# Second cross-attention layer of a two-layer perceiver block: where the full steps issue their value, key and context products

## What is computed

```python
# query = layernorm(x): (2, 256, 256); key = value = ctx_1024: (2, 4096, 256)
Q = proj(query, wq, bq); K = proj(key, wk, bk); V = proj(value, wv, bv)   # 16 heads of 16
energy = einsum('bhqd,bhkd->bhqk', Q, K) / sqrt(16)
attn = softmax(energy, axis=-1)
out = einsum('bhqk,bhkd->bhqd', attn, V)
x = x + out.reshape(B, S, 256) @ wo.T + bo
```

## Time and profile before

| | us |
|---|---|
| median of three runs | 1801.49 |
| the profiled execution's own time | 1800.53 |
| its span | 1798.8 |
| PE busy | 1561.7 |
| DVE busy | 1071.2 |
| ACT busy | 744.7 |
| POOL busy | 503.4 |

### The profile page before, as it was taken

How to read it: one execution, slowest core, us unless ns; L and a number is a source line. 1 busy time by engine, 2 the same in 40 slices (tenths; PEclk the granted TensorE clock), 3 DMA queues, 4 the chain that set the end, 5 groups by cost and what they waited for, 6 DMA issues and landing times. The chain is left out here.

```text
span 1798.8 us, 26051 instructions
## 1 busy us (share of the span) xinstructions
PE 1561.7 (87%) x9943; PEld 1153.8 (64%) x9943; DVE 1071.2 (60%) x1684; ACT 744.7 (41%) x996; POOL 503.4 (28%) x630
## 2 busy tenths in 40 slices
PE   7989999999999668859999687999999899984298
PEld 6767777777877457738888554555565455442288
DVE  6856666666552564345665598777776776016641
ACT  4535555544544132223443111555455455852120
POOL 1005534434569000000000300544444444730000
PEclk9989999999999776759999898999999999996599
DMA  4333333322321100022222122111111110000253
GB/s 164 146 95 100 118 132 104 129 88 90 106 65 42 36 1 1 0 72 94 93 71 92 47 94 94 71 71 48 48 71 71 48 71 1 2 1 24 94 189 103
DMA packets 68527, 134.24 MB, mean 75 GB/s; under 512 B 8722, under 2 KB 38980, under 8 KB 68420
## 3 DMA queue, kind: packets, MB, share of 16 engines
q1 hardware_dynamic: 68228, 132.74, 22.5%
q10 hardware_dynamic: 192, 0.05, 0.0%
HBM read 98.64 MB, written 17.30 MB: 64 GB/s over the span
## 5 line engine op out<-in xcount | busy, mean ns | idle before, releaser
L850 ACT ACTIVATE P<-score 128x1024 f32<-128x1024 f32 x256 | 255.3, 1023 | 169.8 <-PE score L1262 169.8
L641 POOL CAST st<-ef 32x512 fp32r<-32x512 f32 x384 | 235.7, 614 | 313.0 <-PE score L1262 268.7
L1843 DVE TENSOR_REDUCE mx<-bank 128x1 f32<-128x512 f32 x384 | 247.3, 686 | 103.4 <-PE bank L1277 101.9
L1051 PE MATMUL bank<-c_hi,w_split 128*128 128x512 f32 x512 | 178.1, 411 | 19.4 <-ACT arena L947 5.9
L1262 PE MATMUL score<-qs,st 97*128 97x512 f32 x512 | 173.9, 429 | 5.0 <-DMA qs<-shift 3.8
L606 POOL TENSOR_TENSOR sum<-sum,P 128x512 f32<-128x512 f32 x84 | 111.6, 1329 | 192.5 <-ACT P L764 192.5
L764 ACT ACTIVATE P<-score 128x1024 f32<-128x1024 f32 x128 | 129.4, 1025 | 74.1 <-PE score L1087 71.7
L1277 PE MATMUL bank<-ef,qm 128*128 128x512 f32 x384 | 142.3, 431 | 18.5 <-DVE mx L1843 13.7
L1733 DVE TENSOR_REDUCE mx<-bank 128x1 f32<-128x512 f32 x192 | 123.5, 686 | 52.2 <-PE bank L1101 43.9
L1051 PE MATMUL bank<-w_split,c_hi 128*128 128x256 f32 x768 | 147.3, 291 | 0.6 <-ACT v L860 0.6
L1051 PEld LDWEIGHTS bank<-c_hi,w_split 128*128 128x128 f32 x512 | 99.0, 193 | 58.4 <-issue 13.3
(11 more groups left out here) (329 smaller groups left out, 2683.9 us busy)
## 6 DMA issues: line engine op xcount, KB each, us to landing
c_hi<-split_ctx SPq DMA_DIRECT2D x48, 512.0 KB, 3.3
c_lo<-split_ctx SPq DMA_DIRECT2D x48, 512.0 KB, 4.3
w<-k SPq DMA_DIRECT2D x128, 128.0 KB, 3.5
arena<-in_L_ffn_w SPq DMA_DIRECT2D x16, 1024.0 KB, 5.2
arena<-in_L_ffn_W SPq DMA_DIRECT2D x16, 1024.0 KB, 5.4
c_in<-in_ctx SPq DMA_DIRECT2D x16, 512.0 KB, 3.9
split_ctx<-c_hi SPq DMA_DIRECT2D x16, 512.0 KB, 3.6
split_ctx<-c_lo SPq DMA_DIRECT2D x16, 512.0 KB, 4.5
```

What stands on the lines that cost most here:

```text
L641: pool.tensor_copy(st1[32 * block:32 * block + 32, k, :], ef1[rows, g % ERING, part, :].bitcast(F32)).then_inc(a[f"st{k}"], 16)
L850: act.activation(P1[:, index % PRING, :], score[n % 2][:], ACT.Exp).then_inc(a["p"], 1)
L1051: last = mm(dst, l, r, start=(n == 0), stop=(n == len(pairs) - 1))
L1843: v.tensor_reduce(mx1[:, u % 2, i, n:n + 1], bank_of(a, g + 1, f"m{n}")[:], AX.X, ALU.max).then_inc(a["red"], 1)
```

## The change

In the full steps the mixture is issued in two rows of four blocks: row 1 takes the last four blocks of chunk `g - 1`, row 5 the first four of chunk `g`. All six key products come behind row 0, with ACT's copy behind its first weights and DVE's low part behind the reductions of row 1. The values come behind the rows 2 and 4, with ACT's copies behind its third and fifth weights. The instructions are the same in number and size; the steps before 9 and after 32 are as before, and so are the ends of the steps with `i = 0`.

```diff
@@ ACT, cross1
                         weights(g, n)
                         if i and t < CHUNKS:
-                            if n == 3:
+                            if n == 0:
                                 keys(t)
-                            if n in (5, 7) and u % 2 == 0:
-                                values(u, i, n // 2 - 2)
+                            if n in (2, 4) and u % 2 == 0:
+                                values(u, i, n // 2 - 1)
@@ PE, cross1
                         if t <= CHUNKS:
                             maxima(t - 1, n)
-                            if n < 2 and g % NCH:
-                                mixture(g - 1, (4 + 2 * n, 5 + 2 * n))
-                            if n in (4, 6):
-                                mixture(g, (n - 4, n - 3))
+                            if n == 1 and g % NCH:
+                                mixture(g - 1, range(4, 8))
+                            if n == 5:
+                                mixture(g, range(4))
...
                         if i and t < CHUNKS:
-                            if n in (2, 3):
-                                keys(t, (n - 2,))
-                            if n in (5, 7) and u % 2 == 0:
-                                values(t, n // 2 - 2)
+                            if n == 0:
+                                keys(t)
+                            if n in (2, 4) and u % 2 == 0:
+                                values(t, n // 2 - 1)
@@ DVE, cross1
-                        if (t < LAG and h == 1) or (i and LAG <= t < CHUNKS and h == 4):
+                        if (t < LAG and h == 1) or (i and LAG <= t < CHUNKS and h == 1):
                             low_keys(t)
```

## The result

The changed kernel takes 1822.2 us (median of four runs, 1813.69 to 1823.91) against 1800.8 for the kernel before: ratio 1.0108, 95% interval 1.0075 to 1.0141. It is slower, by 21.4 us where 15.4 were forecast; the median lies at the upper end of the range, 0.2 us above it. The profiled execution took 1822.17, its span is 1820.5.

The account below looks back on a forecast made before the run. How PE's rows line up with DVE's reductions through two banks of maxima bounds the kernel, not any engine's sum. Row prices summed over the stage gave 15.4 us on 1800.5, so 1816 us, range 1805 to 1822.

Parts of the forecast that it names:

- The cause: Full steps: merging two mixture rows saves 0.29 us if the emptied row needn't wait; it waits 0.70 or 0.32.
- The prices of rows: PE's rows in full steps: four blocks 2.99 us, whole keys 2.32, values 2.36, empty 1.66 behind filled, 1.28 behind empty.
- The sum of the full steps: All gains and losses of the stage's steps, from row 1 to row 1, added up: 15.4 us slower.
- Low parts of queries: DVE's work behind row 7's reductions, 1.68 us: delays steps by 0.67, against 0.90 before without values, 0.22 with them.
- Behind a division: Behind steps 17 and 25 DVE's division, 6.6 us, sets the time to the next row 1 before and after alike.
- The steps 15, 23 and 31: They end in row 0 of a step without keys there, 1.04 us less: in all -1.2 us.
- the steps 16 and 24: Rows 1 to 7 take 11.86 us against 10.96 before, 0.9 us lost in each.
- the clock, "So I count nothing": PE's short stops of 0.3 to 0.7 us in the steps leave the granted clock full: nothing added.
- faster rival: Full steps: DVE keeps ahead, emptied rows take 0.96 us, 45 mergers save 0.29 each, 13 us: 1787 us; chance 0.08.
- clock rival: Runs of three empty rows drop the clock once in each of 14 steps, 3.4 us each: 1863 us; chance 0.03.

Follow-up runs that it names:

- the parts alone: Kernel before with only the mixture in fours, 1823.6 us; or with only keys, values and low part of the keys moved, mixture in pairs, 1828.7 us.
- faster reductions: DVE's reductions of maxima in full steps cut to 256 of 512 columns: kernel before 1778.2 us, changed kernel 1774.9 us.
- a third bank: Changed kernel, but in steps without values maxima may also use the bank of the keys and values, order of instructions unchanged: 1798.0 us.
- the old order with a third bank: Kernel before, but in steps without values maxima may also use the bank of the keys and values in some rows: 1784.4 us.
- the seam filled: Eight small zero products behind the scores of each of rows 0 to 3 of step 33: changed kernel 1817.8 us, old order with a third bank 1784.5.
- the mixture alone: Kernel before with only the mixture in fours in rows 1 and 5, keys, values and low part of the keys as before: 1823.6 us, ratio 1.0109.

## Why the prediction was right, and by how much not

**The cause** was right: the mergers saved less than the emptied rows wait. The prices of rows hold for whole steps in every order tried: 15.46 and 17.62 forecast, 15.44 and 17.59 measured; the parts alone within 0.1 us. They were got by subtraction, and no empty row of 1.66 can be read by itself: behind the long row 1 the empty rows take 1.18, 1.41 and 1.29, and the next filled row takes the rest. What shows the cause is taking the scarcity away: with faster reductions the loss is gone, and with a third bank the changed kernel's steps without values fall from 15.44 to 14.39. The third bank does not turn the sign, though, once the kernel before has it too. Of other engines the table of waits shows one new wait of PE in the steps, six times for ACT's copy of the values (PEld L1291 <- ACT v L860, 2.2 us in all); the rows where it stands last 2.98, as priced. PE's waits for DVE grew by 35.7 us where I said some 25.

**The sum of the full steps** was 15.4 and measured 16.3 us, with errors that cancel; that it came so near is in part luck. *Low parts of queries*: I counted 0.67 in the new place; it is 0.35 (15.79 - 15.44, 17.94 - 17.59). DVE's two instructions took 1.32 there, not 1.68. Such a pair takes 0.87 where POOL is idle (from 1039.14 in the kernel before) and 1.22 to 1.69 in the full steps, always beside POOL's copies; with the same code around it the kernel before shows 1.22 in the steps 9 to 11 and 1.69 in step 12, and in step 28 the old order with a third bank took 14.75 us with a pair of 1.68 and, with the seam filled, 14.32 with one of 1.22. So how DVE and POOL happen to meet seems to set it; no run tests that. And the 15.96 that I took for a step with such a delay before holds for the steps 12, 27 and 28 alone; 10, 11, 13 and 29, which the delay reaches too, take some 15.5. In place of 0.17 each, 10 and 11 lose 0.3, and 12, 27 and 28 gain 0.17. *Behind a division*: the steps 18 to 22 lose 4.5, not 6.8; 1.0 of the difference is the low parts, the rest lies in step 18, which loses nothing. Its first rows run at the lower clock in both kernels, but for longer before (us, PE, PEld, DVE, ACT, POOL, PEclk, DMA, GB/s; rows 1 and 2 before, row 1 after):

```profile
1274.07:1280.90 6.83, 6.83 (x27) 3.97 (x28) 3.12 (x5) 1.02 (x1) 1.59 (x3) 0.53 0.00 0
...
1281.06:1285.85 4.79, 4.79 (x37) 2.15 (x38) 2.49 (x4) 0.00 (x0) 0.37 (x1) 0.64 0.00 0
```

By the granted clock that is some 6.4 us at the lower level against 3.4; half of the difference, 1.5 us by my estimate, is about what step 18 does not lose. Behind the other division it is the other way round, and step 26 loses 1.0. The steps 15, 23 and 31 gain 2.2, not 1.2.

**What I had too low** are the steps 16 and 24: from row 1 to the next row 1 they lose 2.3 and 3.9 us, of which the prices give 0.9 for their own rows and 0.7 for the whole keys in the row 0 that follows. I had left out two things: an empty row 7 ends later than its first product shows (0.5 us more to the first scores of step 25), and the clock: from the first scores of step 25 to the maxima of its row 1 it takes 4.4 us (1407.03 to 1411.47), at full clock in step 17 it took 2.96.

**The term that was mis-sized most** is the clock, "So I count nothing". The rows that I read for it were right for the steps of the changed kernel: short waits for DVE, 200 of them now, did not lower its clock (1.00 from 1220 to 1260 and from 1380 to 1400). The Trainium skill tells of a kernel whose clock swung between its two levels as PE idled briefly between groups of products ("TensorE: Matmul & The Clock Gate", section "A second HAM failure mode: psum-queue depth-cycling"); the changed kernel's trace doesn't show that in its steps, that of the mixture alone shows two such falls. But the seams between units were not in my sum. There the clock fell in the changed kernel and not in the one before: some 1.5 us at step 25, which are in the 16.3, and 2.7 behind step 32; with the seam filled 2.1 of them were gone. The 0.9 by which the full steps exceed the sum, these 2.7, the 2.1 of the later stages and 0.6 ahead of the stage are what lies between 1816 and 1822.

The **faster rival** was right that DVE has time to spare and wrong that PE can use it: it comes true only where reductions are quick, and then by half. The **clock rival** named the right resource in the wrong place: in the changed kernel the clock fell at the seams, not in the steps. With the mixture alone it did fall in two steps, behind such a run of empty rows.

## What to carry to other kernels

When two engines hand work over through two buffers, rows of the one in sequence are on average no shorter than a turn of the other (1.18, 1.41 and 1.29 us here against 1.29 for a pair of reductions), and a long row pays nothing forward: price a new order row by row, by what each row carries and whether the one before was empty, and check the prices on whole steps before using them. Putting like work together empties other rows. Here it paid only where the other engine was made faster, by 7.0 us in the full steps; one buffer more shortened both orders and left the old one ahead. The third buffer by itself was worth 16 us without moving a single instruction.

## What was not expected of the hardware

The granted clock at the seams differs between kernels whose code there is the same: behind step 32 it was full in the kernel before and in the changed one with a third bank, and at its lower level for a part of the seam in the changed kernel, which took 2.7 us longer. In the steps 10 and 12 of the mixture alone it fell, in the steps 11, 27 and 28 with the same wait for DVE it didn't. In both kernels with eight products of zeros behind each of four rows of scores it was full there; whether because of them, two profiles don't settle.
